# A graph network on one core: the first edge pass gets its source one-hots from two engines, and the first block's loads change queue

## What is computed

```python
h = jnp.concatenate([x[row], edge_attr], axis=1)
h = jnp.maximum(h @ W1a + b1a, 0.0) @ W1b + b1b
ssum = jax.ops.segment_sum(h, col, num_segments=x.shape[0])
...
mean = jnp.where(cnt > 0, ssum / jnp.maximum(cnt, 1.0), 0.0)
```

## Time and profile before

| | us |
|---|---|
| median of 3 runs | 3633.37 (3633.12 to 3634.44) |
| the profiled execution, device time | 3635.56 |
| its span in the trace | 3633.8 |
| PE, DVE, ACT, POOL busy | 2789.7, 2949.4, 1525.8, 1358.0 |
| first edge pass, first to last add of an edge part | 1776.11 to 2200.70 |

### The profile page before, as it was taken

How to read it: one execution, slowest core, us unless ns; L and a number is a source line. 1 busy time by engine, 2 the same in 40 slices (tenths; PEclk the granted TensorE clock), 3 DMA queues, 4 the chain that set the end, 5 groups by cost and what they waited for, 6 DMA issues and landing times. The chain is left out here.

```text
span 3633.8 us, 77596 instructions
## 1 busy us (share of the span) xinstructions
PE 2789.7 (77%) x25482; PEld 2031.7 (56%) x25482; DVE 2949.4 (81%) x6844; ACT 1525.8 (42%) x3073; POOL 1358.0 (37%) x1260
## 2 busy tenths in 40 slices
PE   2098989970474376177699997899999699979994
PEld 1065666640122022022699996466666699969994
DVE  9899999979698998999677774655554799968887
ACT  2455655650352253154699994333333200022221
POOL 0066666651686375286000000455554000024440
PEclk9999999985797698599799998999999699989997
DMA  8978777774796496398477661322222243324441
GB/s 286 418 231 221 219 199 214 213 208 153 220 296 195 128 295 216 94 294 258 146 218 226 217 210 38 76 67 68 68 67 56 56 109 105 96 69 110 115 110 35
DMA packets 449003, 601.16 MB, mean 165 GB/s; under 512 B 84997, under 2 KB 333635, under 8 KB 448621
## 3 DMA queue, kind: packets, MB, share of 16 engines
q1 hardware_dynamic: 402817, 505.88, 45.8%
q0 software_dynamic: 39424, 78.61, 7.2%
q10 hardware_dynamic: 6380, 11.77, 1.1%
HBM read 359.53 MB, written 230.75 MB: 162 GB/s over the span
## 5 line engine op out<-in xcount | busy, mean ns | idle before, releaser
L1211 PE MATMUL psum<-a_probs,z 128*65 128x512 f32 (+1 forms) x1050 | 438.7, 557 | 156.7 <-DVE a_probs L1107 156.7
L1850 DVE TENSOR_SCALAR rp_hot_dst<-rp_ramp,slot_key 128x696 bf16<-128x696 f16 x900 | 300.2, 403 | 221.8 <-PE psum L1994 221.8
L907 POOL DMA_INDIRECT slots<-bc_rec,idx x400 | 388.1, 970 | 211.4 <-issue 107.2
L605 POOL DMA_INDIRECT slots<-h,idx x256 | 344.2, 1345 | 303.0 <-DMA h<-recs 232.8
L1143 ACT ACTIVATE a_tops<-a_tops,a_s_low 128x512 f32<-128x512 f32 (+2 forms) x300 | 283.4, 946 | 296.4 <-DVE a_tops L1098 285.3
L1211 PEld LDWEIGHTS psum<-a_probs,z 128*65 128x65 f32 x1050 | 122.7, 140 | 468.2 <-DVE a_probs L1107 302.9
L1827 POOL DMA_INDIRECT rp_fetch<-piece_rows,slot_row x283 | 279.0, 986 | 240.6 <-PE psum L1994 183.2
L1107 DVE SCALAR_TENSOR_TENSOR a_probs<-a_tops,a_counts 128x512 f32<-128x512 f32 (+2 forms) x300 | 288.8, 964 | 34.6 <-issue 22.5
L1098 DVE SCALAR_TENSOR_TENSOR a_tops<-table,a_s_rest,big 128x512 f32<-128x512 f32 (+2 forms) x300 | 306.4, 1024 | 3.9 <-DMA big<-shift_rows 3.1
L1922 ACT ACTIVATE rp_msg<-psum 128x192 bf16<-128x192 f32 (+1 forms) x456 | 176.1, 386 | 303.4 <-PE psum L1968 298.8
L1985 PE MATMUL psum<-rp_hot_dst,rp_msg 128*128 128x512 bf16 x1234 | 258.2, 313 | 2.6 <-ACT rp_by_relation L1933 1.4
(11 more groups left out here) (461 smaller groups left out, 6753.4 us busy)
## 6 DMA issues: line engine op xcount, KB each, us to landing
slots<-big SPq DMA_DIRECT2D x60, 1012.5 KB
ep_rec<-slots SPq DMA_DIRECT2D x60, 1012.5 KB, 5.8
a_counts<-edge_counts SPq DMA_DIRECT2D x75, 538.5 KB, 4.4
a_counts<-edge_counts SPq DMA_DIRECT2D x150, 256.0 KB, 4.5
a_counts<-edge_counts SPq DMA_DIRECT2D x75, 512.0 KB
edge_counts<-bc_counts SPq DMA_DIRECT2D x12, 3125.0 KB
hot_rows<-ep_hot_src SPq DMA_DIRECT2D x300, 96.0 KB
sp_hot_src<-hot_rows SPq DMA_DIRECT2D x300, 96.0 KB
```

The costliest lines, as they stand in the source:

```text
L605: pool.indirect_dma_start(k.slots, bass.IndirectOffsetOnAxis(k.idx[:, at:at + 1], 0), self.rows[y][:, t, :], None).then_inc(self.scattered ...
L907: pool.indirect_dma_start(k.slots, bass.IndirectOffsetOnAxis(k.idx[:, first + t:first + t + 1], 0), rec[:, j, t, :], None).then_inc(scatte ...
L1211: last = nc.tensor.matmul(sums[:, a:b], k.z[:, s, 0:D + 1], probs[:, a:b], start=s == 0, stop=True, skip_group_check=True)
L1850: v.tensor_scalar(hot_dst[:, q % HOT_SLOTS, :], ramp[:, :], k.slot_key[:, q:q + 1], None, ALU.is_equal)\
```

## The change

In `edge_slots`, x and the 36 weights are issued from ACT's list, ahead of everything else there, and SP waits for both to have landed before it issues the first clearing DMA.

In the first edge pass the spelling is gone. PE turns `slot_lo` of a whole batch with one matmul (`turn_lo`), ACT copies the 15x128 result to fp16 (`copy_lo`), and POOL stores it to `lo_rows` in memory, waits until it has landed, and loads it back onto all partitions into one of three places in `k.big` (`spread_lo`: 3.75 KB stored, 480 KB written to SBUF a batch). Of every three chunks, DVE makes the one-hot of two by one comparison (`match_source`), and ACT makes the third with square and relu (`raise_source`). Both work five chunks ahead, in round c for chunk c + 5. The ring keeps its eight places and its condition (`wait_hot_free`). There are six record buffers in the place of five, and DVE describes a batch four batches ahead.

```diff
@@ -315,10 +316,9 @@
                 sp.dma_start(src_i[:, :], d["src_rank"]).then_inc(loaded, 16)
                 sp.dma_start(type_i[:, :], d["type_rank"]).then_inc(loaded, 16)
                 sp.dma_start(w[:, :], d["weight_rank"]).then_inc(loaded, 16)
-                sp.dma_start(k.x[:, :, :], d["x"].rearrange("(t p) f -> p t f", p=P)).then_inc(x_in, 16)
-                for to, source in parts:
-                    sp.dma_start(to, source).then_inc(weights_in, 16)
                 sp.wait_ge(cleared, 1)
+                sp.wait_ge(x_in, 16)
+                sp.wait_ge(weights_in, 16 * len(parts))
                 per = SLOTS * FILL * REC
                 flat = k.big[:, :, :].rearrange("p t c -> p (t c)")
                 for c in range(0, NCHUNK, FILL):
@@ -327,6 +327,9 @@
 
             @block.scalar
             def _(act):
+                act.dma_start(k.x[:, :, :], d["x"].rearrange("(t p) f -> p t f", p=P)).then_inc(x_in, 16)
+                for to, source in parts:
+                    act.dma_start(to, source).then_inc(weights_in, 16)
                 act.wait_ge(ends_ready, 1)
                 act.dma_start(att.ends[0, :].rearrange("(p t) -> p t", t=7), low[:, :]).then_inc(ends_out, 16)
                 act.dma_start(att.ends[1, :].rearrange("(p t) -> p t", t=7), high[:, :]).then_inc(ends_out, 16)
...
@@ -1266,10 +1269,19 @@
 
 
     nc = k.nc
-    LOADS, READ_AHEAD = Ring.RECORD_LOADS, 3
-    SPELL_AHEAD, LOOK_AHEAD = 6, 3
+    LOADS, READ_AHEAD, FIRST_READ = Ring.RECORD_LOADS, 4, 3
+    HOT_AHEAD, LOOK_AHEAD = 5, 3
+    edges = kind == "edges"
+    LO_SLOTS, BATCHES = 3, NCHUNK // FILL
+    READ_AT = {b: (b - READ_AHEAD) * FILL for b in range(READ_AHEAD + 1, BATCHES)}
+    READ_AT.update({FIRST_READ: 1, READ_AHEAD: 3})
+    READ_IN = {c: b for b, c in READ_AT.items()}
+    raised_here = lambda c: c % 3 == 2
+    RAISED = [c for c in range(NCHUNK) if raised_here(c)]
+    MATCHED = [c for c in range(NCHUNK) if not raised_here(c)]
+    raised_to = lambda c: sum(x <= c for x in RAISED)
...
+            lo_t = sb("lo_t", [FILL * SLOTS, 2, P], FP16)
+            lo_all = k.big[:, :, :].rearrange("p t c -> p (t c)").bitcast(FP16)[:, 0:LO_SLOTS * FILL * SLOTS * P]\
+                .rearrange("p (y c) -> p y c", y=LO_SLOTS)
...
-        def key_bank(n):
-            return k.psum[:, n % KEY_BANKS, 0:SLOTS * P]
+        def turned_bank(b):
+            return k.psum[0:FILL * SLOTS, b % KEY_BANKS, 0:P]
+
+        def lo_chunk(c):
+            part = c % FILL * SLOTS * P
+            return lo_all[:, c // FILL % LO_SLOTS, part:part + SLOTS * P]
+
+        def wait_lo(eng, c):
+            eng.wait_ge(lo_in[c // FILL % LO_SLOTS], 16 * (c // FILL // LO_SLOTS + 1))
...
+        def wait_hot_free(eng, c):
+            if c >= HOT_SLOTS:
+                eng.wait_ge(looked_up, c - HOT_SLOTS + 1)
+                eng.wait_ge(hot_io[c % HOT_SLOTS], 16 * (c // HOT_SLOTS))
 
         def row_bank(n):
...
                     for c in range(b * FILL, (b + 1) * FILL):
-                        sp.wait_ge(hot_made, c + 1)
+                        wait_hot(sp, c)
                         sp.dma_start(k.hot_rows[c, :, :], hot_src[:, c % HOT_SLOTS, :]).then_inc(hot_io[c % HOT_SLOTS], 16)
 
...
+                def spread_lo(b):
+                    pool.wait_ge(lo_copied, b + 1)
+                    nc.gpsimd.dma_start(k.lo_rows[b, :].rearrange("(t p) -> t p", p=P), lo_t[:, b % 2, :]).then_inc(lo_kept, 16)
+                    pool.wait_ge(lo_kept, 16 * (b + 1))
+                    if b >= LO_SLOTS:
+                        last = (b - LO_SLOTS + 1) * FILL - 1
+                        pool.wait_ge(hot_matched, matched_to(last))
+                        pool.wait_ge(hot_raised, raised_to(last))
+                    nc.gpsimd.dma_start(lo_all[:, b % LO_SLOTS, :], k.lo_rows[b, :].partition_broadcast(P))\
+                        .then_inc(lo_in[b % LO_SLOTS], 16)
+
+                if edges:
+                    for b in range(READ_AHEAD + 1):
+                        spread_lo(b)
                 if aside:
                     aside(nc.gpsimd)
                 ring.wait_rows(pool)
...
+                def match_source(c):
+                    wait_lo(dve, c)
+                    wait_hot_free(dve, c)
+                    v.tensor_scalar(hot_src[:, c % HOT_SLOTS, :], lo_chunk(c), k.lane[:, 0:1], None, ALU.is_equal)\
+                        .then_inc(hot_matched, 1)
...
                 if edges:
-                    for b in range(READ_AHEAD):
+                    for b in range(FIRST_READ):
                         describe(b)
                 dve.wait_ge(left_in, 16)
                 left_number()
+                if edges:
+                    for c in range(HOT_AHEAD):
+                        if not raised_here(c):
+                            match_source(c)
                 if kind == "near":
                     weigh(0)
                 for c in range(NCHUNK):
-                    if edges and c % FILL == 0 and c // FILL + READ_AHEAD < NCHUNK // FILL:
-                        describe(c // FILL + READ_AHEAD)
+                    if edges and c in READ_IN:
+                        describe(READ_IN[c])
+                    if edges and c + HOT_AHEAD < NCHUNK and not raised_here(c + HOT_AHEAD):
+                        match_source(c + HOT_AHEAD)
                     hot_target(c)
                     if kind == "near" and c + 1 < NCHUNK:
...
-                def square_key(c):
-                    act.wait_ge(spelled, c + 1)
-                    if c >= 2:
-                        act.wait_ge(hot_made, c - 1)
-                    nc.scalar.activation(square[:, c % 2, :], key_bank(c), ACT.Square, bias=k.minus_lane[:, 0:1])\
+                def copy_lo(b):
+                    act.wait_ge(lo_turned, b + 1)
+                    if b >= 2:
+                        act.wait_ge(lo_kept, 16 * (b - 1))
+                    nc.scalar.activation(lo_t[:, b % 2, :], turned_bank(b), ACT.Copy).then_inc(lo_copied, 1)
+
+                def raise_source(c):
+                    n = raised_to(c) - 1
+                    wait_lo(act, c)
+                    if n >= 2:
+                        act.wait_ge(hot_raised, n - 1)
+                    nc.scalar.activation(square[:, n % 2, :], lo_chunk(c), ACT.Square, bias=k.minus_lane[:, 0:1])\
                         .then_inc(squared, 1)
-
-                def hot_source(c):
-                    act.wait_ge(squared, c + 1)
-                    if c >= HOT_SLOTS:
-                        act.wait_ge(looked_up, c - HOT_SLOTS + 1)
-                        act.wait_ge(hot_io[c % HOT_SLOTS], 16 * (c // HOT_SLOTS))
-                    nc.scalar.activation(hot_src[:, c % HOT_SLOTS, :], square[:, c % 2, :], ACT.Relu, bias=k.ones[:, 0:1],
-                                         scale=-1.0).then_inc(hot_made, 1)
+                    wait_hot_free(act, c)
+                    act.wait_ge(squared, n + 1)
+                    nc.scalar.activation(hot_src[:, c % HOT_SLOTS, :], square[:, n % 2, :], ACT.Relu, bias=k.ones[:, 0:1],
+                                         scale=-1.0).then_inc(hot_raised, 1)
...
+                for c in range(NCHUNK):
                     if c in FETCH_NO:
                         weigh_fetched(c)
-                    ahead = c + SPELL_AHEAD - 1
-                    if edges and c >= 0:
+                    if edges:
                         rectify(c)
-                    if edges and 0 <= ahead < NCHUNK:
-                        square_key(ahead)
-                    if edges and 0 <= ahead - 1 < NCHUNK:
-                        hot_source(ahead - 1)
+                        if c - 1 in READ_IN:
+                            copy_lo(READ_IN[c - 1])
+                        if c + HOT_AHEAD < NCHUNK and raised_here(c + HOT_AHEAD):
+                            raise_source(c + HOT_AHEAD)
...
-                def spell(c):
-                    pe.wait_ge(described, c // FILL + 1)
-                    if c >= KEY_BANKS:
-                        pe.wait_ge(squared, c - KEY_BANKS + 1)
-                    for s in range(SLOTS):
-                        at = c * SLOTS + s
-                        last = nc.tensor.matmul(key_bank(c)[:, s * P:(s + 1) * P], k.slot_lo[:, at:at + 1].broadcast_to([P, P]),
-                                                k.ident16[:, :], start=s == 0, stop=True, skip_group_check=True)
-                    last.then_inc(spelled, 1)
+                def turn_lo(b):
+                    pe.wait_ge(described, b + 1)
+                    if b >= KEY_BANKS:
+                        pe.wait_ge(lo_copied, b - KEY_BANKS + 1)
+                    nc.tensor.matmul(turned_bank(b), k.slot_lo[:, b * FILL * SLOTS:(b + 1) * FILL * SLOTS], k.ident16[:, :],
+                                     start=True, stop=True).then_inc(lo_turned, 1)
...
-                    if KEY_BANKS and c + SPELL_AHEAD < NCHUNK:
-                        spell(c + SPELL_AHEAD)
```

(8 more changed lines are left out.)

27 lines of the change are left out of this document (22 added, 5 removed).

## The result

The changed kernel takes **3787.2 us** (median of 4 runs, 3784.2 to 3789.9) against 3633.9 for the kernel before in the same comparison: a ratio of **1.0418, 95% interval 1.0405 to 1.0431**, 4.2% slower. The prediction was 3743 with a range of 3670 to 3825.

The account below looks back on a forecast made before the run. No engine bounds the whole kernel; PE and ACT are at their limit in the first edge pass. Pass +98, its start +6 and first block +6 gave +110 on 3635.56, less 2.2: 3743 us, range 3670 to 3825.

Parts of the forecast that it names:

- PE and ACT are relieved: First edge pass: PE falls from 1.39 to about 1.2 us a chunk; ACT does one square and relu in three chunks.
- the ring's cover: First edge pass: one-hot stores had about 11 us before needed; now three rounds, at most 3.6 us, so DVE waits.
- The first rival: First edge pass: store lands within DVE's three rounds, PE sets the pace, kernel ends faster at 3590 us; chance 0.10.
- Landing of the first store: First edge pass: a batch's first one-hot store lands behind the records' load, 6.15 + 0.4 for source rows = 6.5 us.
- Two rounds behind it: First edge pass: DVE's rounds between that landing and SP's next batch, 1.87, 2.08 or 1.39 by kind, mean 1.78 us.
- The loop: First edge pass: store landing plus two DVE rounds, 6.5 + 1.8 = 8.3 us a batch against 6.95; bounds 7.2 to 9.2.
- Placing: First edge pass: SP places ten triples ahead of the load, no longer covered, 3.9 us each, 39 us in all.
- The last batch and 25 chunks: End of the first edge pass: the last of 54 batches at 8.3 us, then 25 chunks at 1.2 = 30 us.
- Start of the pass: Start of the first edge pass: slot numbers first go to memory and back, +6 us, between 3 and 12.
- First block: First block: tile ends land late at 47, DVE ends at 177 against 171.96, +6 us in all, bounds -2 to +20.
- Rival 2: First edge pass: source rows' round trip through memory bounds it, 15.3 us a batch, about 4080 us; chance 0.02.
- The rule that was weighed against the loop: Skill's rule that completion is not FIFO per issuing engine: the store would not hold DVE; the prediction kept its waits.

Follow-up runs that it names:

- three ways: Changed kernel with stores ahead of the load (1.0223), stores as soon as made (1.0195), or 13 places for one-hots (1.0089), each as ratio to the kernel before.
- the second trace: The changed kernel unaltered, run again in the second group of experiments: pass 565.6 us, ratio to the kernel before 1.0379.

## Why the prediction was right, and by how much its terms were off

- **PE and ACT are relieved, and the ring's cover is gone: right.** The wait named for DVE is the first in the list, and taking its cause away (three ways) takes 71 to 129 us off the pass. The first rival (the store lands in time) and with it the reading that small stores overtake is refuted: DVE waited for one 47 times in 53 batches.
- **Landing of the first store, 6.5 us: too small.** It is 7.25. The spreading was taken at 0.4 of its bounds 0 to 1.2, "since a load that takes 5.8 us leaves gaps"; against the run without it, it costs 0.8 (7.25 - 6.44; 0.6 by the second trace). The rest of the landing was 6.15; it is 6.2 in 33 batches without spreading and 6.44 with the six late ones. What the step had wrong is that it priced the spread load by its size alone. Its price goes by when it starts: nothing, or 2.1 us, where the upper bound was 1.2.
- **Two rounds behind it, 1.78: near.** 1.97. By kind they are 2.3, 2.0 and 1.6 us, where 2.08, 1.87 and 1.39 were forecast. The comparison itself is not the reason: it was costed at 0.21 us, and DVE's next instruction starts 0.24 us after it (2013.88 to 2014.12).
- **The loop, 8.3: 9.25.** The 53 distances of the loads add up to 525.2 us (1777.90 to 2303.09), where 53 x 8.3 + 39 = 479 was forecast: +46. This is the mis-sized term, 0.95 us a batch: 0.75 of landing and 0.2 of rounds. It is just above my upper bound of 9.2. The time stayed inside the range because the high end had the other terms at their bounds too.

```profile
1777.90 0.38 SPq L2403 DMA_DIRECT2D ep_rec<-slots  x1
...
2303.09 0.38 SPq L2403 DMA_DIRECT2D ep_rec<-slots  x1
```

- **Placing, 39: right** (35 by distance in the changed kernel, 39 by moving it).
- **The last batch and 25 chunks, 38.3: right.** From 2303.09 to the end of the last sum, 2341.6, it is 38.5.
- **Start of the pass, +6: right** at +5.2.
- **First block, +6: wrong, +0.4.** The clearing began at 31.45 in place of 33.72 as forecast, but the ends landed at 42.25 and not at 47. DVE was 5.6 us late and not 10, and DVE's slack of 5.3 us behind SP took up all but 0.3 of it. The landing beside the clearing was costed from POOL's 14.14 us under the full clearing; these loads were issued as it began.
- **The join, +7.4: not in the sum.** A price of POOL's 120 DMAs behind the pass, where I had only looked for their place in it.
- **Rival 2** (POOL's trip bounds the pass) is not what happens. DVE waited for the spread rows twice, 12.7 us in all, both at the start of the pass. The Trainium skill (SBUF — State Buffer, section on two separate sides) says that GpSimd cannot write the descriptors of its DMAs while VectorE runs an operation in a 2-port mode. No run here shows whether DVE's comparisons are of that kind; POOL's DMAs of 480 KB landed 5.7 us after their issue (median) beside them.
- **The rule that was weighed against the loop.** The store comes 0.4 us behind the records in the earlier trace rows, and 0.2 to 0.45 us behind them in 44 of the 53 batches of the changed kernel. The prediction quoted from the Trainium skill (DMA: Bandwidth & Descriptors, section on queues, rings and completion order) that completion is not in order for an issuing engine; the page draws this for a later DMA on one engine behind one on 16. The same paragraph says that a semaphore's increment lands only after every earlier write of that DMA engine, across its queues. In the trace the store's semaphore climbs in 16 steps over about half a microsecond and is full only behind the records, in all 53 batches, as this rule has it for a store that runs on all 16 engines. Read in full, the rule speaks for the loop. It would also let a spread load on another queue hold the store back: in the other nine batches the store comes 1.1 to 1.7 us behind the records, and in each of them the spread load had started within 0.8 us of theirs.

Together: 110 + 46 (the loop) + 7 (the join) - 6 (the block) - 1 (the start) + 2 (the first chunks, 7.6 us in place of 5.4) = 158. Less the further 11 us in the stage ahead, which no step explains, it is 147, where the profiled execution has 148. So part of the nearness to the forecast is luck: those 11 us, and a term for the block that was 6 too high, hide 17 of the 55 us by which the loop, the join and the first chunks cost more.

## What to carry to other kernels

A buffer ring has two ends: before an engine is given work on it, count how many rounds lie between the event that frees a place and the instruction that needs it, on the engine's own list, and compare that with a whole landing behind whatever is ahead in the queue. Do this for each kind of round: where two engines share the work, the instruction that needs the place can stand ahead of the event that closes the loop in one batch and behind it in the next, and moving it across gave five times what one round is worth (3.76 us against 0.74). Look at the landings one by one before you take their mean: here a transfer on another queue cost nothing or 2 us, by when it started. And when one loop is opened, ask which transfer has the next shortest distance; in these runs its landing was longer than it had been (7.5 us against 5.8).
